# Attention and mixture-of-experts block: plain fp32 scores, row maxima over zero-padded queries, mask rows by DMA, new instruction orders

## What is computed

```python
q = ln @ Wq.T
kv = concatenate([xn @ Wkv.T, ln @ Wlkv.T], axis=1)      # 256 context rows, then 256 own rows
k, v = kv[..., :128], kv[..., 128:]                       # split into 2 heads of 64
qn, kn = rmsnorm(q, qn_g) * 64**-0.5, rmsnorm(k, kn_g)
attn = einsum('bhid,bhjd->bhij', qn, kn)
attn = softmax(where(full_mask, attn, -max_float), axis=-1)
x = x + tanh(g_xattn[0]) * (merge_heads(attn @ v) @ Wo.T + bo)

gates = sigmoid(xt @ expert_sel.T); keep the 4 largest of 32 per row, 0 for the others
scores = relu(einsum('nd,edf->nef', xt, keys)) * gate[:, :, None]    # 32 experts of 64
x = x + tanh(g_ffn[0]) * einsum('nef,efv->nv', scores, values)
```

## Time and profile before

| | us |
|---|---|
| median of 3 runs | 118.26 |
| lowest, highest | 118.08, 122.36 |
| the profiled execution | 117.8 |
| its span, first to last instruction | 116.0 |

### The profile page before, as it was taken

How to read it: one execution, slowest core, us unless ns; L and a number is a source line. 1 busy time by engine, 2 the same in 40 slices (tenths; PEclk the granted TensorE clock), 3 DMA queues, 4 the chain that set the end, 5 groups by cost and what they waited for, 6 DMA issues and landing times.

```text
span 116.0 us, 2124 instructions
## 1 busy us (share of the span) xinstructions
PE 107.1 (92%) x672; PEld 87.4 (75%) x672; DVE 98.7 (85%) x315; ACT 60.3 (52%) x136; POOL 15.5 (13%) x26
## 2 busy tenths in 40 slices
PE   4579999999999989989989699999999999999990
PEld 4478998776799768869979565776788888888860
DVE  5779999799979999888697797896989999999952
ACT  4698999955784385054371412005453634455420
POOL 6030000290004026000053250000000000000000
PEclk9999999999999999999999999999999999999999
DMA  3789600000000000000002996353437676681002
GB/s 86 209 250 418 285 0 6 3 0 0 0 0 6 0 0 0 8 0 0 0 13 87 278 286 245 114 214 146 117 134 243 254 234 208 198 222 49 0 0 90
DMA packets 7047, 12.77 MB, mean 110 GB/s; under 512 B 829, under 2 KB 2493, under 8 KB 6782
## 3 DMA queue, kind: packets, MB, share of 16 engines
q1 hardware_dynamic: 7038, 12.66, 33.4%
HBM read 12.00 MB, written 0.66 MB: 109 GB/s over the span
## 4 chain that ended last, share of the span: by engine, by line
PE 87%; DVE 8%; issue 2%; ACT 1%; DVEq 0%
PE bank L729 12%; PE bank L731 12%; PE bank L730 12%; PE bank L873 11%; PE bank L927 6%; PE bank L738 4%; PE bank L759 4%; PE bank L799 3%; PE bank L788 3%; PE bank L827 3%; PE bank L854 2%; PE bank L766 2%; DVE shift_l L376 2%; PE bank L813 2%; PE bank L856 1%
## 5 line engine op out<-in xcount | busy, mean ns | idle before, releaser
L545 DVE SCALAR_TENSOR_TENSOR keys<-bank,inT 128x512 f32<-128x512 f32 x32 | 21.3, 685 | 2.3 <-PE bank L731 1.3
L706 ACT ACTIVATE hid_hi<-keys 128x512 fp32r<-128x512 f32 x24 | 15.0, 631 | 14.3 <-DVE keys L545 7.4
L562 DVE TENSOR_TENSOR hid_lo<-keys,hid_hi 128x512 fp32r<-128x512 f32 x24 | 16.1, 687 | 0.9 <-ACT hid_hi L706 0.8
L873 PE MATMUL bank<-vw,prob 128*128 128x129 f32 x128 | 15.9, 278 | 0.0
L873 PEld LDWEIGHTS bank<-vw,prob 128*128 128x128 f32 x128 | 14.8, 192 | 0.7 <-issue 0.7
L729 PE MATMUL bank<-xm_hi,k_lo 128*128 128x512 f32 x32 | 14.8, 462 | 0.0
L731 PE MATMUL bank<-xm_hi,k_hi 128*128 128x512 f32 x32 | 12.6, 393 | 0.0
L730 PE MATMUL bank<-xm_lo,k_hi 128*128 128x512 f32 x32 | 12.5, 391 | 0.0
L455 DVE CUSTOM_DVE_ANT_0 junk<-bank,mask_b 128x512 bf16<-128x512 f32 x16 | 10.4, 686 | 0.9 <-PE bank L827 0.7
L738 PE MATMUL bank<-ident 128*128 128x128 f32 x48 | 9.4, 341 | 1.5 <-POOL ident L318 1.5
L675 ACT ACTIVATE prob<-bank 128x512 f32<-128x512 f32 x16 | 8.6, 591 | 2.9 <-PE bank L860 2.9
(11 more groups left out here) (136 smaller groups left out, 224.4 us busy)
## 6 DMA issues: line engine op xcount, KB each, us to landing
inT<-gate_rows SPq DMA_DIRECT2D x32, 256.0 KB, 3.7
keys<-keys_in SPq DMA_DIRECT2D x1, 1024.0 KB, 6.8
values<-values_in SPq DMA_DIRECT2D x1, 1024.0 KB, 8.9
out<-x_mid SPq DMA_DIRECT2D x4, 128.0 KB, 2.3
vecs_x<-x_in SPq DMA_DIRECT2D x1, 256.0 KB, 4.5
wa<-wa_in SPq DMA_DIRECT2D x1, 208.0 KB, 3.0
cx<-ctx_in SPq DMA_DIRECT2D x2, 96.0 KB, 2.9
cx<-ctx_in SPq DMA_DIRECT2D x1, 192.0 KB, 4.8
```

Of the source, the lines that this page charges most:

```text
L545: dve.scalar_tensor_tensor(hid[:, n % 3, :], bank[H_BANK[n % len(H_BANK)]][:, :], 0.0, gated[:, n % SLOTS, :], ALU.max, ALU.mult).then_inc ...
L562: dve.tensor_tensor(hid_lo[:, m % RING, :], hid[:, n % 3, :], hid_hi[:, m % RING, :].bitcast(F32), ALU.subtract).then_inc(hid_lo_ready, 1)
L706: act.activation(hid_hi[:, m % RING, :], hid[:, n % 3, :], ACT.Copy).then_inc(hid_hi_ready, 1)
L873: last = pe.matmul(bank_of(b, OUT + t)[:, WOA * a:WOA * a + WOA], prob[:, b % 2, a, j, P * t:P * t + P], vw[:, b, j, a, :], start=(j == 0) ...
```

## The change

Scores: `turn_qk` on ScalarE now writes `qT` and `kT` in plain fp32, and `weights` makes one fp32 product for each head in place of three fp32r ones. VectorE's `turn_qk` with its low parts is gone.

Row maxima: a new step `round_qk` on ScalarE rounds `qT` and `kT` to fp32r. The rounded q of each head lies in a tile of 128 partitions of its own, with zeros in the partitions of the other head (two memsets on GpSimd, once), so `row_max` is a product over all 128 rows. That tile shares its memory with `hid_lo`.

Mask: the two rows of `shift_l` that hold the mask are copied by two DMAs of SyncE behind the load of the values, not by VectorE.

Values: `WHOLE` is 4, so chunks 4 to 7 of the first half are split products too.

Orders: all three lists are new. Cut to the core:

```diff
-WHOLE = 8
+WHOLE = 4
...
+        qT_hi = hid_lo[:, :, :].rearrange("p i n -> p (i n)").rearrange("p (b a s) -> p b a s", b=B, a=HEADS)
...
+            sp.wait_ge(shift_ones_ready, 1)
+            sp.wait_ge(mask_ready, 1)
+            sp.wait_ge(open_ready, 1)
+            for row in range(32, SH, DH):
+                sp.dma_start(shift_l[row:row + 1, :, :], mask_b[row:row + 1, :, :]).then_inc(shift_mask_ready, 16)
...
+            for a in range(HEADS):
+                pool.memset(qT_hi[DH - DH * a:P - DH * a, :, a, :].bitcast(F32), 0.0).then_inc(pads_ready, 1)
+                pool.wait_ge(pads_ready, a + 1)
...
-            def shift_mask():
...
-            def turn_qk(b):
-
-                dve.wait_ge(qk_hi_ready, 2 * b + 1)
-                dve.scalar_tensor_tensor(qT_lo[:, b, :], bank_of(b, TURN_QK + 1)[:, 0:S], gq[:, :],
-                                         qT_hi[:, b, :].bitcast(F32), ALU.mult, ALU.subtract).then_inc(qk_lo_ready, 1)
...
-                act.activation(kT_hi[:, b, :], bank_of(b, TURN_QK)[:, :], ACT.Copy, scale=vec(V_KG)).then_inc(qk_hi_ready, 1)
+                act.activation(kT[:, b, :], bank_of(b, TURN_QK)[:, :], ACT.Copy, scale=vec(V_KG)).then_inc(qkT_ready, 1)
+
+            def round_qk(b):
+                act.wait_ge(qkT_ready, 2 * b + 1)
+                for a in range(HEADS):
+                    rows = slice(DH * a, DH * a + DH)
+                    act.activation(qT_hi[rows, b, a, :], qT[rows, b, :], ACT.Copy).then_inc(qk_hi_ready, 1)
+                act.wait_ge(qkT_ready, 2 * b + 2)
+                act.activation(kT_hi[:, b, :], kT[:, b, :], ACT.Copy).then_inc(qk_hi_ready, 1)
...
-                    pe.matmul(bank_of(b, ROW_MAX + i)[:, :], qT_hi[rows, b, P * t:P * t + P], kT_hi[rows, b, :],
+                    pe.matmul(bank_of(b, ROW_MAX + i)[:, :], qT_hi[:, b, a, P * t:P * t + P], kT_hi[:, b, :],
...
-                        pe.matmul(o[a], kT_lo[rows[a], b, keys_t], qT_hi[rows[a], b, :], start=False, stop=False)
-                    for a in range(HEADS):
-                        pe.matmul(o[a], kT_hi[rows[a], b, keys_t], qT_lo[rows[a], b, :], start=False, stop=False)
-                    for a in range(HEADS):
-                        last = pe.matmul(o[a], kT_hi[rows[a], b, keys_t], qT_hi[rows[a], b, :], start=False, stop=True)
+                        last = pe.matmul(o[a], kT[rows[a], b, keys_t], qT[rows[a], b, :], start=False, stop=True)
...
-    warm 0, warm 1, warm 2, warm 3, warm 4, warm 5, turn_in 0, warm 6, warm 7, warm 8, warm 9, project 0,
+    warm 0, warm 1, warm 2, warm 3, warm 4, warm 5, warm 6, warm 7, warm 8, warm 9, warm 10, warm 11, warm 12,
+    warm 13, warm 14, warm 15, warm 16, warm 17, turn_in 0, warm 18, warm 19, warm 20, project 0, turn_in 1,
```

More of the change, by code:

```diff
@@ L86 @@
+    up 1.11, split 1.10, up 1.12, up 1.13, split 1.11, split 1.12, up 1.14, split 1.13, up 1.15, split 1.14,
+    split 1.15, finish 0, finish 1
 """
 ACT_ORDER = """
-    stats_in 0, norm_in 0, constants 0, stats_in 1, turn_in 0, norm_in 1, project 0, turn_in 1, split_keys 0,
-    sum_qk 0, fold 0, project 1, stats_in 2, stats_in 3, vlat 0, turn_qk 0, split_keys 1, vctx 0, sum_qk 1,
-    norm_in 2, vlat 1, norm_in 3, vctx 1, turn_in 2, turn_in 3, turn_qk 1, vlat 2, vctx 2, project 2, sum_qk 2,
@@ new lines @@
+    weights 0.0, sum_qk 2, vlat 3, vctx 3, split_keys 1, weights 0.1, project 3, turn_qk 2, sum_qk 3, round_qk 2,
+    split_keys 2, weights 1.0, turn_qk 3, split_values 0, round_qk 3, split_keys 3, split_values 1, weights 1.1,
+    stats_mid 0, weights 2.0, turn_mid 0, weights 2.1, stats_mid 1, weights 3.0, select 0, turn_mid 1,
+    split_values 2, select 1, weights 3.1, turn_gates 0, turn_gates 1, split_values 3, stats_mid 2, turn_mid 2,
+    stats_mid 3, select 2, turn_res 0, split 0.4, split 0.5, turn_mid 3, split 0.6, split 0.7, turn_gates 2,
@@ L374, in shift_ones @@
             def shift_ones():
[L376 to L383 removed]
+                dve.memset(shift_l[:, :, :], 1.0).then_inc(shift_ones_ready, 1)
             def scale_wo():
```

100 lines of the change are left out of this document (44 added, 56 removed).

## The result

The changed kernel took 116.5 us (median of four runs, 115.99 to 116.64) against 118.23 for the kernel before in the same comparison: a ratio of 0.985, with a 95% interval of 0.9811 to 0.9889. The forecast was 118.5 us in a range of 115.0 to 123.9. The time lies in the range, and the gain is under the 2% from which it was to be called "faster", but the direction was wrong: a gain of 1.5% that the measurement tells clearly from none, where a small loss was forecast. The profiled execution took 116.57 us for a span of 114.8; before it was 117.8 for 116.0, so their whole difference of 1.2 us lies within the span.

What follows compares the result with a forecast made beforehand. TensorE's own work was taken to bound the kernel, VectorE next. From the profiled 117.8 us, terms of +2.7, +0.3, -0.7, +0.4, -1.0 and -1.0 gave 118.5 us, range 115.0 to 123.9.

Steps and rivals of the forecast that it cites:

- Term 1: Score products, 16 key tiles: one fp32 product per head takes 0.65 us a tile for 0.48, +2.7 us (bounds +1.1, +8.2).
- The rival that the heads don't overlap: Score products: fp32 records of the two halves run one after another, 0.99 us a tile, 123.9 us in all; chance 0.20.
- the one on the second record's weight load: Score products: a head's second record waits some 0.1 us for its weights, 121 us in all; chance 0.06.
- Term 2: Eight row-maximum pairs on full rows, 0.46 us each, and fewer changes of row group: +0.3 us.
- Term 3: Experts' part: four more value chunks as split products save TensorE 0.7 us; VectorE's lateness adds 0.4.
- The bound of 2.4: Upper bound on lateness from the four added split chunks, in us: all four of VectorE's added subtractions exposed.
- Term 4: TensorE's waits behind the front: shift_r -0.8, xm_lo -1.0, down 0.0 +0.5, row_max 2.1 +0.3; -1.0 us (bounds -1.8, +1).
- Term 5: The front: three delays against fewer warm-ups behind turn_in 0, weights 0.0 at 27.8 for 28.84, -1.0 us (bounds -3.5, +1.5).
- All three delays: Front: VectorE's stats_in 1 before norm_in 0, ScalarE's constants (bo load) before norm_in 0, ScalarE's added round_qk; bound +1.5 us.
- ScalarE holds the row maxima: Front: round_qk loads ScalarE, TensorE idles at row_max, front +1.1 us instead of -1.0, 120.6 us in all; chance 0.12.
- Faster: VectorE's relief and missing warm-ups count fully, front -3.5 us, tile nearer 0.60 us; 115.2 us in all, chance 0.18.
- The mask rows and the earlier residual transposes at 0: Mask rows copied by DMA and residual transposes standing earlier on TensorE: each forecast to change the time by 0.

## Why the prediction was right or wrong

The terms, as forecast and as the runs and the two traces give them:

| term | forecast | found |
|---|---|---|
| 1, score products | +2.7 | +0.8 to +1.2 |
| 2, row maxima and row groups | +0.3 | 0 to +0.3, what is left |
| 3, four more split chunks | -0.7, and +0.4 for lateness | -0.7, by the count of products |
| 4, waits behind the front | -1.0 | -1.2 |
| 5, the front | -1.0 | -0.16 (-0.6 by the means of three) |
| not forecast | | -0.3 |
| sum, by the two traces | +0.7 | -1.2 |

**Term 1 failed, by its size, and it alone turns the sign.** The step was "Started in that order, record 1 of head 1 can run only beside record 2 of head 0", from which 0.65 a tile followed. The records of both heads start together, at 28.80 and again at 29.01 to 29.03, and they do so even when head 1 is issued behind three records of head 0. The tile is at the lower bound, 0.55, and the run with this part alone has 0.8 to 1.2 us for all sixteen, not 2.7. The rival that the heads don't overlap fell with it, and so did the one on the second record's weight load: a head's second record starts 0.22 us after its first, as on full rows. The 1.5 us or more by which the term was too high are most of the 1.9 us between forecast and result.

**Term 2 was right in its parts, not in its sum.** The half-row pair between full-row steps is 0.43, as read from the earlier trace rows; the full-row pair is 0.56, where 2 x 0.23 = 0.46 was put. The 0.1 us between is as large as what a half-row pair was held to lose ahead of it, so the three pairs that stand alone won nothing. Half-row maxima would be 0.3 to 0.4 us cheaper in the new orders. What the term comes to against the kernel before is only a balance: the attention stages changed by +0.53, of which +0.8 to +1.2 is term 1 and -0.6 the wait for `shift_r`; that leaves 0 to +0.3.

**Term 3's gain is there, and its lateness isn't where it was put.** No run measured it by itself: both that tried changed what limits the experts' part. The stretch from `up 0.0` to the last `down` went from 49.35 to 47.87. Of these 1.48 us, 1.0 is the wait for `xm_lo`, and the wait for `keys` takes 0.4 back; 0.9 is left, of which 0.7 are the four chunks by the count and 0.2 aren't explained. The last residual transposes, two products that now stand ahead of the last `down` and not behind it, take another 0.2 of the stretch, so 0.4 stay unexplained. The bound of 2.4 was a real danger: in the old lists the stretch was 2.5 us longer with these chunks than the count says. In the new ones VectorE is busy for 46.59 of 49.6 us (43.9 before), and TensorE doesn't wait for it behind `down 0.0`.

**Term 4 was right.** The wait for `xm_lo` fell away, that for `shift_r` mostly, and 0.4 at `down 0.0` came, as 0.5 had been put. That step on TensorE in the kernel after:

```profile
66.80 1.95 PE L925 MATMUL bank<-keys,values 128*128 128x512 f32 x4 [0.38 <-DVE keys L541]
```

The 0.3 us at `row_max 2.1` are there, but they are nothing new. The weight load of its second product, in the kernel after:

```profile
39.76 0.19 PEld L829 LDWEIGHTS bank<-kT_hi,hid_lo 128*128 128x128 f32 x1 [0.42 <-DVE mx L451]
```

It starts 0.61 us behind the first one, since VectorE had not yet taken the maxima before. The view of waits doesn't list it for TensorE's products, since by the profile the first one is still draining in that time. In the kernel before, the same load came at 38.31 with a wait of 0.38 us for VectorE.

**Term 5 was wrong, by 0.8 us between the two traces and by 0.4 by the means of three.** All three delays were named, and the first real steps were forecast near where they came: the copy of `turn_in 0` at 10.0 (found 10.24), `project 0` at 10.4 (10.95), `row_max 0.0` at 22.5 (23.08), `weights 0.0` at 27.8 (28.68). The load of `bo` let ScalarE go at 8.28, not 7.98, and about half a microsecond from there is carried through to the row maxima. From there to `weights 0.0` it is 5.6 us where 5.3 was put, and three pairs of row maxima lie in it, each 0.1 us dearer than in term 2. ScalarE's part at the row maxima, in the kernel after:

```profile
21.44 0.84 ACT L669 ACTIVATE hid_lo<-qT 64x256 fp32r<-64x256 f32 x2
22.30 0.63 ACT L671 ACTIVATE kT_hi<-kT 128x512 fp32r<-128x512 f32 x1
```

Their product starts at 23.08, when `kT_hi` is there. The two halves and k take 1.5 us from the first start to the last one's end, 1.2 had been put. So the rival "ScalarE holds the row maxima" had a real mechanism: TensorE waits 0.4 us there. Its 1.1 us in the front didn't come in the new orders; with the old lists the front is 2.3 us longer, for all parts of the change together.

**The rival "Faster" had the right sign for partly the right reason.** The tile came out at 0.55, under its 0.60. The missing warm-ups didn't count in full: the front gave 0.2 to 0.6 us, not 3.5. That 116.5 lies within the forecast's own range, 116 to 120.5, is luck in part: term 1 was at least 1.5 us too high, and term 5, up to 0.8 us too low, hid some of it.

**The mask rows and the earlier residual transposes at 0:** the first is worth 0.25 us by itself. The second wasn't tried alone; the tail behind the last `down` shrank by 0.1 us.

## What to carry to other kernels

Products in two row groups that appear as two records each ran side by side here in both orders of issue; the order of issue was no reason for a middle value between the bounds. Before a step is moved to an engine that has room on average, look at what is queued directly behind it in that engine's list: with the rounding directly behind `turn_qk` and the old lists the front was 2.3 us longer than before, with the new lists it was no longer at all. And a change of order earns its gain only with the buffers that allow it: who frees a buffer, and how far down its list that engine must have come, decides whether a producer can run ahead.

## What the runs showed of the hardware

- Two plain fp32 products in rows 0 to 63 and 64 to 127 run at once: four records in the time of two, 0.55 us for a tile of 256 columns with its shift product. With the order of issue changed it is 0.55 as well.
- GpSimd's conversion of the mask (1.09 us) held up a VectorE instruction that overlapped with it: a pair that takes 0.60 us took 1.32. It happened in seven of the ten traces that have the conversion in its first place, by when the mask was loaded. In five of them it hit an instruction on a few columns, which took 0.77 to 1.06 us and takes 0.16 otherwise. The trace of the kernel before is not one of the seven. In the three traces with the conversion held back nothing was hit.
- TensorE doesn't always reach its pace at the same place. In the run with the four split chunks in the old orders the first products of `project 0` took 2.05 us for four, which take 1.10 in the kernel after, and those of `project 1` were still as slow at 16.34. The timeline of that run:

```profile
9.81 2.05 PE L759 MATMUL bank<-wa,inT 128*128 128x256 f32 x4 [0.53 <-ACT inT L620]
11.65 1.06 PE L766 MATMUL bank<-wa,inT 96*128 96x128 f32 x4
...
16.34 1.91 PE L759 MATMUL bank<-wa,inT 128*128 128x256 f32 x4
```

The kernel before has the same list on TensorE up to there and took 1.52 for the first of them, with the pace changing in between. In the run with the mask rows alone, the same list again, the two products of `turn_in 0` already take 0.44 us at 6.38. So the faster pace came before 6.4 us, at about 10 and at 19 in three executions of one list. The view of stretches puts the granted clock at 1.00 for 5 to 20 us of that run; the durations are what shows the slower pace, twice that of the faster one, as 1.2 is to 2.4 GHz. Its `weights 0.0` came at 33.37, 4.5 us after that of the kernel before. What decides where it ends was not tried.
